# Packing the turned values of two head groups, one sum matmul, and a later setup in a fused attention and feed-forward kernel

## The chip, the cores and the metric

The kernel runs on one core of one Trainium2 chip. The metric is the device time of one execution in microseconds (us), less is better. The engines are TensorE (PE in the profile, with its weight loads as PEld), VectorE (DVE), ScalarE (ACT), GpSimd (POOL) and SyncE (SP), which issues all DMAs here.

## The reference

Sixteen batches of 256 tokens with 128 features go through one post-norm transformer layer. Everything is float32 at the interfaces.

```python
def _genetic_fitness(g):                       # per head, T x 8
    corr = g g^T / (|g_i| |g_j| + 1e-8)
    corr = (corr * m + 1) / 2                  # m: causal band of 128
    denom = mean_j(corr) + 0.5
    fit = 1 / (denom * sum_i(1 / denom))       # the sum runs over the 256 tokens
    return softmax(where(m, corr * fit, -1e10))
# attention
g, v = x @ Wg.T + bg, x @ Wv.T + bv            # 16 heads of 8
x = layernorm(x + (fitness(g) @ v) @ Wo.T + bo)
# feed-forward: inputs and weights quantised to FP4 in blocks of 16
gate, up = fp4(x) @ fp4(w_gate).T, fp4(x) @ fp4(w_up).T     # 352 wide
x = layernorm(x + fp4(silu(gate) * up) @ fp4(w_down).T)
```

## The kernel before

Each engine has its own instruction stream, written out by hand, and the streams meet in semaphores. All streams run the same loop of rounds, `t` from -3 to 20. Round `t` computes the scores and exponentials of batch `t`, and beside them the early steps of batches `t+1` to `t+3` and the late steps of batches `t-1` to `t-4`. So the order in each stream is fixed: an instruction that waits holds everything behind it on its engine.

For a batch the steps are these. TensorE makes genes and values in bank WA (L787, and the gene bias by L789); ScalarE squares and copies them (L603, L608); VectorE sums to squared lengths and seeds a reciprocal square root (`seed`), which GpSimd refines in twelve small steps (`newton`, L437 to L444). VectorE scales the genes (`gh`), GpSimd and VectorE split them into two 16-bit halves (A16: L495, L1159). TensorE takes window sums (L799), VectorE turns these into `rden`, the reciprocal of the denominator for 2 x 16 columns (two token tiles of 16 heads). TensorE sums `rden` over the tokens (L819, two matmuls that accumulate the two tiles), VectorE takes the reciprocal (`rtot`, L1095) and the fitness, which scales the genes again (Bf, L1109; B16: L488, L1125). A16 and B16 are turned on TensorE (L716) and copied to AT and BT by ScalarE (L570, L582).

The scores of two heads at a time go to bank S (L668 adds the mask, L672 the products), ScalarE takes exponentials to Pm (L531). `values(x, c)` multiplies the Pm of head group `c` (four heads) with gv (L689): each head has 9 columns that matter (8 values and a column of ones for the sum) in a slot of 32, and the result is turned, with heads along the partitions. Groups 0 and 1 lie beside each other in bank OT as two regions of 256 columns, so do 2 and 3, and ScalarE copies each pair to OTs (`values_out`, L544, 512 columns). `values_back` turns them back with the picking matrix `pick`, one matmul for each group and token tile, into bank WA (L703), where VectorE divides (L1146, L1152). Then come the projection (L828), the first norm, FP4 quantisation of x, gate and up (L709, L710), tanh, quantisation of h, its turn (L743), down (L761) and the second norm.

Setup before the first round: TensorE computes the bias rows and a combined output bias (L640 to L642) and VectorE copies them to `bias`; GpSimd splits this into three bf16 rows (L393 to L404) and builds masks and `pick`. The FP4 quantisation of the three weight matrices (`weights_to_scale` to `weights_scaled` on VectorE, over 1120 columns) and their turn on TensorE (`turn_weights`) stand in rounds -2 and -1.

## Time and profile before

| | us |
|---|---|
| median of 3 runs | 452.44 (451.97 to 454.86) |
| the profiled execution | 455.05 |
| span in its profile, first to last instruction | 453.3 |
| PE busy in the span | 363.7 (80%) |
| DVE busy | 273.4 (60%) |
| ACT busy | 229.6 (51%) |
| POOL busy | 179.1 (40%) |
| mean granted TensorE clock | 0.882 of full speed |

The span is what the profile shows; 1.75 us of the profiled execution lie outside it. The granted clock has two levels, 0.5 (1.2 GHz) and 1.0 (2.4 GHz). Times in rows are microseconds from the start of the span. A matmul in float32 is shown as two passes, each with its own weight load, so eight picking matmuls stand as x16.

### The profile page before, as it was taken

To read this page: it belongs to the slowest core of one execution; us is meant where nothing else is said; L and a number is where in the kernel's file an instruction comes from. 1 tells how busy PE (TensorE), PEld (TensorE's weight loads), DVE (VectorE), ACT (ScalarE), POOL (GpSimd) and SP (SyncE) were. 2 spreads that over 40 slices of the span, in tenths; PEclk is the share of its full clock that TensorE was granted. 3 is DMA by queue.
4 is the path that set the end of the run, shared out by engine and by line. 5 is a ranking of instruction groups with operands and counts; after the bars stand their busy time and mean duration, and the time that the engine had idled before them with its cause. 6 is when DMAs were issued, how large, how long until landed. Compare 5 with 4: busy or idle time off the path is not lost.

```text
span 453.3 us, 9200 instructions
## 1 busy us (share of the span) xinstructions
PE 363.7 (80%) x3121; PEld 226.8 (50%) x3121; DVE 273.4 (60%) x804; ACT 229.6 (51%) x498; POOL 179.1 (40%) x464
## 2 busy tenths in 40 slices
PE   1425887798898989898898989898999989966552
PEld 1214344454656565656465656555656564654242
DVE  0565123335547776768686768575656657888661
ACT  1101555627346657575757475657274647633121
POOL 4743230404224636353645354626152323325241
PEclk9999589959589999899999899989696969998555
DMA  3100000000000101010101010100000000000000
GB/s 88 35 1 23 2 13 0 25 1 23 1 21 5 37 1 37 1 36 4 35 1 36 3 35 1 37 1 25 0 25 2 25 0 25 2 12 13 12 2 25
DMA packets 12407, 7.66 MB, mean 17 GB/s; under 512 B 1027, under 2 KB 12357, under 8 KB 12357
## 3 DMA queue, kind: packets, MB, share of 16 engines
q1 hardware_dynamic: 12356, 7.03, 5.5%
q8 instruction: 26, 0.43, 0.4%
q14 instruction: 25, 0.20, 0.2%
HBM read 4.93 MB, written 2.10 MB: 16 GB/s over the span
## 4 chain that ended last, share of the span: by engine, by line
PE 71%; ACT 11%; issue 7%; DVE 6%; POOL 3%; DMA 0%; SPq 0%; ACTq 0%; POOLq 0%; DVEq 0%
PE OT L689 12%; PE S L668 9%; PE WA L703 8%; PE WD L761 7%; PE S L672 7%; PE WC L709 6%; PE WD L710 5%; PE WB L716 4%; PE WA L787 4%; ACT AT L570 3%; ACT Pm L531 3%; ACT xaT L596 2%; PE WB L828 2%; PE WA L819 2%; ACT y L537 1%
## 5 line engine op out<-in xcount | busy, mean ns | idle before, releaser
L531 ACT ACTIVATE Pm<-S 128x384 f32<-128x384 f32 x256 | 111.9, 492 | 107.9 <-PE S L672 107.2
L668 PE MATMUL S<-mask,ident 128*128 128x384 f16 x256 | 68.9, 354 | 10.0 <-ACT Pm L531 8.4
L461 POOL TENSOR_TENSOR hq<-hm,hs 128x352 f32<-128x352 f32 x32 | 25.2, 788 | 96.9 <-DVE hm L1036 96.8
L689 PE MATMUL OT<-Pm,gv 128*32 128x256 f32 (+1 forms) x1024 | 60.6, 359 | 0.0
L672 PE MATMUL S<-BT,AT 32*128 32x256 f16 (+1 forms) x512 | 45.7, 258 | 0.0
L1012 DVE SCALAR_TENSOR_TENSOR hh<-th,WC 128x352 f32<-128x352 f32 x32 | 16.7, 522 | 44.2 <-ACT th L549 44.2
L689 PEld LDWEIGHTS OT<-Pm,gv 128*32 128x32 f32 x1024 | 28.3, 115 | 22.5 <-issue 7.8
L709 PE MATMUL WC<-wguT,xaT 128*128 128x352 f32 x64 | 29.5, 544 | 11.7 <-ACT xaT L596 7.1
L672 PEld LDWEIGHTS S<-BT,AT 32*128 32x128 f16 x512 | 14.6, 94 | 45.8 <-issue 45.8
L703 PE MATMUL WA<-pick,OTs 128*128 128x36 f32 x256 | 36.7, 306 | 0.0
L668 PEld LDWEIGHTS S<-mask,ident 128*128 128x128 f16 x256 | 19.0, 100 | 34.2 <-issue 16.3
L703 PEld LDWEIGHTS WA<-pick,OTs 128*128 128x128 f32 x256 | 35.6, 222 | 0.2 <-issue 0.2
L437 POOL TENSOR_TENSOR nt<-seed 128x32 f32<-128x32 f32 x16 | 4.8, 303 | 77.4 <-DVE seed L982 77.4
L761 PE MATMUL WD<-wdT,hqT 128*128 128x128 f32 (+1 forms) x192 | 33.8, 341 | 1.8 <-ACT hqT L577 1.8
L544 ACT ACTIVATE OTs<-OT 128x512 f32<-128x512 f32 x32 | 19.2, 599 | 29.0 <-PE OT L689 29.0
L761 PEld LDWEIGHTS WD<-wdT,hqT 128*128 128x128 f32 (+1 forms) x192 | 30.3, 245 | 5.6 <-ACT hqT L577 2.8
L716 PE MATMUL WB<-ident,B 128*128 128x128 f16 x128 | 11.5, 241 | 24.0 <-ACT AT L570 17.2
L1125 DVE TENSOR_TENSOR B<-Bf,B 128x512 f16<-128x512 f32 x16 | 11.1, 692 | 27.0 <-POOL B L488 27.0
L787 PE MATMUL WA<-wgv,xT 128*128 128x256 f32 x64 | 22.2, 481 | 5.2 <-issue 4.2
L710 PE MATMUL WD<-wguT,xaT 128*128 128x352 f32 x64 | 26.0, 490 | 0.0
L1146 DVE RECIPROCAL orec<-WA 128x32 f32<-128x32 f32 x16 | 5.7, 358 | 33.6 <-PE WA L703 33.6
L455 POOL TENSOR_TENSOR hn<-h,hrn 128x352 f32<-128x352 f32 x32 | 25.1, 793 | 1.4
(142 smaller groups left out, 714.5 us busy)
## 6 DMA issues: line engine op xcount, KB each, us to landing
xT<-x_turned_dram SPq DMA_DIRECT2D x16, 128.0 KB, 2.3
x_res<-x_dram SPq DMA_DIRECT2D x16, 128.0 KB, 2.2
out_dram<-yo SPq DMA_DIRECT2D x16, 128.0 KB, 2.1
wf<-w_down_dram SPq DMA_DIRECT2D x1, 176.0 KB, 2.6
wgv<-wgv_dram SPq DMA_DIRECT2D x1, 128.0 KB, 2.0
wf<-w_gate_dram SPq DMA_DIRECT2D x1, 128.0 KB, 2.2
wf<-w_up_dram SPq DMA_DIRECT2D x1, 128.0 KB, 2.2
woT<-wo_dram SPq DMA_DIRECT2D x1, 64.0 KB
```

Of the source, the lines that this page charges most:

```text
L455: pool.tensor_tensor(b3(hn[:, k]), b3(h[:, k]), bc(hrn[:, k], QB), ALU.mult).then_inc(s_hn, 1)
L461: pool.tensor_tensor(b3(hq[:, k, 0:I]), b3(hm[:, k]), bc(hs[:, k], QB), ALU.mult).then_inc(s_hq, 1)
L531: act.activation(Pm[:, group % PR, hd % 4, :], S[:, (H * x + hd) % 3, 0:SCW], ACT.Exp, scale=1.0 / ZS).then_inc(s_exp, 1)
L668: pe.matmul(S[:, bank, 0:SCW], ident16[:, :], mask16[:, :], start=True, stop=False)
L672: i = pe.matmul(S[:, bank, q0:q1], AT[r:r + 32, x % 2, c, kt * P:(kt + 1) * P], BT[r:r + 32, x % 2, c, T - (q1 - q0):T], start=False, stop ...
L689: i = pe.matmul(OT[VP * g:VP * (g + 1), col + T - (q1 - q0):col + T], gv[:, x % GVR, kt, H + 4 * c + g, :], Pm[:, (GROUPS * x + c) % PR, g ...
L703: i = pe.matmul(WA[:, o:o + 4 * OW], OTs[:, c // 2, T * (c % 2) + n * P:T * (c % 2) + (n + 1) * P], pick[:, :, :].rearrange("p g e -> p (g ...
L709: pe.matmul(WC[:, 0:I], lhs, wguT[:, 0:I], start=True, stop=True)
L710: pe.matmul(WD[:, 0:I], lhs, wguT[:, I:2 * I], start=True, stop=True).then_inc(s_gu, 1)
L716: i = pe.transpose(WB16[:, c * T + n * P:c * T + (n + 1) * P], src[:, n * H + 4 * c:n * H + 4 * c + 4].rearrange("p h r d -> p (h r d)"), ...
L761: i = pe.matmul(WD[:, k * D:(k + 1) * D], hqT[0:kn, k, n * P:(n + 1) * P], wdT[0:kn, n, :], start=(n == 0), stop=(n == 2))
L787: pe.matmul(WA[:, k * 2 * D:(k + 1) * 2 * D], xT[:, (t + 3) % 2, k * P:(k + 1) * P], wgv[:, :], start=(k == 0), stop=False)
```

## The change

Three things are done. First, the two groups of a pair now share one region of 256 columns in OT. For an odd group the stationary operand is taken from `gv_flat` 9 columns earlier, so that its 9 columns land on rows 9 to 17 of each slot of 32, and all four accumulating steps of the pair form one sum; the zeros of gv are set one head further. `values_out` copies 256 columns, and `values_back` does one matmul with 72 columns for each pair and token tile: four for each batch in place of eight with 36.

Second, `rden` is summed over tokens with both tiles side by side in one matmul of 32 columns, and VectorE adds the two halves in an instruction of its own (`tot`) before the reciprocal. The aggregation of the first norm now stands ahead of the fitness.

Third, the setup is moved. The gene matmuls of batch 0 are TensorE's first work; for batches 0 and 1 the bias is added by a float32 matmul from `bgrow`. The bias rows are computed in round -3, and split by GpSimd in round -2 (`constants`) after its half of A16 of batch 0; the fill of gv stands in round -1. The weights are scaled at the end of round -1, quantised at the end of round 0, and turned in round 1, in two parts.

```diff
@@ setup, SyncE and GpSimd @@
+            sp.dma_start(xT[:, 0, :], x_turned[0]).then_inc(ld_x[0], 16)
             sp.dma_start(wgv[:, :], wgvT).then_inc(ld_w, 16)
-            sp.dma_start(xT[:, 0, :], x_turned[0]).then_inc(ld_x[0], 16)
-            sp.dma_start(bgrow[:, :], bg.rearrange("(a n) -> a n", a=1)).then_inc(ld_b, 16)
+            sp.dma_start(bgrow[:, :], bg.rearrange("(a n) -> a n", a=1)).then_inc(ld_w, 16)
...
-                pool.memset(gv[:, :, :, H:2 * H, OW:VP], 0.0).then_inc(c_pool, 1)
+                pool.memset(gv[:, :, :, H - 1:2 * H, OW:VP], 0.0).then_inc(c_pool, 1)
...
-                if t == -2:
-                    values_rest()
...
+                if t == -2:
+                    constants()
+                if t == -1:
+                    values_rest()
@@ ScalarE @@
-                act.activation(OTs[:, half, :], OT[:, :], ACT.Copy).then_inc(s_ot, 1)
+                act.activation(OTs[:, half, :], OT[:, 0:T], ACT.Copy).then_inc(s_ot, 1)
@@ TensorE, values and values_back @@
-                        i = pe.matmul(OT[VP * g:VP * (g + 1), col + T - (q1 - q0):col + T],
-                                      gv[:, x % GVR, kt, H + 4 * c + g, :], Pm[:, (GROUPS * x + c) % PR, g, q0:q1],
-                                      start=(kt == 0), stop=(kt == 1))
+                        at = VP * (2 * H * (NT * (x % GVR) + kt) + H + 4 * c + g) - OW * (c % 2)
+                        i = pe.matmul(OT[VP * g:VP * (g + 1), T - (q1 - q0):T], gv_flat[:, at:at + VP],
+                                      Pm[:, (GROUPS * x + c) % PR, g, q0:q1],
+                                      start=(kt == 0 and c % 2 == 0), stop=(kt == 1 and c % 2 == 1))
...
-                    for c in range(GROUPS):
-                        o = (n * H + 4 * c) * OW
-                        i = pe.matmul(WA[:, o:o + 4 * OW], OTs[:, c // 2, T * (c % 2) + n * P:T * (c % 2) + (n + 1) * P],
-                                      pick[:, :, :].rearrange("p g e -> p (g e)"), start=True, stop=True)
+                    for half in range(2):
+                        o = (n * H + 8 * half) * OW
+                        i = pe.matmul(WA[:, o:o + 8 * OW], OTs[:, half, n * P:(n + 1) * P],
+                                      pick[:, :, :, :].rearrange("p c g e -> p (c g e)"), start=True, stop=True)
@@ TensorE, rounds @@
+                if t == 1:
+                    turn_gate_up_weights()
...
+                    if t < -1:
+                        pe.matmul(genes, onesf[0:1, :], bgrow[:, :].rearrange("p (a d) -> p a d", a=1)
+                                  .to_broadcast([1, NT, D]), start=False, stop=True).then_inc(s_gv, 1)
...
-                    for k in range(NT):
-                        i = pe.matmul(WA[:, 0:H], onesf[:, :], rden[:, k * H:(k + 1) * H],
-                                      start=(k == 0), stop=(k == NT - 1))
-                    i.then_inc(s_sum, 1)
+                    pe.matmul(WA[:, 0:NT * H], onesf[:, :], rden[:, :], start=True, stop=True).then_inc(s_sum, 1)
@@ VectorE @@
-                    dve.reciprocal(rtot[:, :], WA[:, 0:H]).then_inc(s_fit, 1)
+                    dve.tensor_reduce(tot[:, :], WA[:, 0:NT * H].rearrange("p (n h) -> p h n", n=NT), AX.X, ALU.add)\
+                        .then_inc(s_fit, 1)
...
+                if t == -1:
+                    weights_to_scale()
+                if t == 0:
+                    weights_exponent()
+                    weights_round()
+                    weights_grid()
                     weights_scaled()
-                if t == -1:
-                    weights_turned()
+                if t == 1:
+                    down_weights()
```

TensorE at the start of the program. Before, the bias rows stand ahead of the genes of batch 0:

```order
L640 MATMUL WC<-bgrow,onesf 128x128 [waits c_dve,ld_b,c_pool]
L641 MATMUL WC<-woT,bvrep 128x128
L642 MATMUL WC<-borow,onesf 128x128
L787 MATMUL WA<-wgv,xT 128x256 [waits ld_x0,c_pool,ld_w]
L787 MATMUL WA<-wgv,xT 128x256
L789 MATMUL WA<-bias16,ones16 128x2x128
```

Now, the same place:

```order
L813 MATMUL WA<-wgv,xT 128x256 [waits ld_x0,ld_w,c_pool]
L813 MATMUL WA<-wgv,xT 128x256
L817 MATMUL WA<-bgrow,onesf 128x2x128
L654 MATMUL WC<-bgrow,onesf 128x128 [waits c_dve,ld_b]
L655 MATMUL WC<-woT,bvrep 128x128
L656 MATMUL WC<-borow,onesf 128x128
```

The genes went ahead of the bias rows, and their last matmul reads `bgrow` instead of the split bias.

VectorE at the turn from round 0 to round 1. `wq_u`, `wq_m` and `wf` belong to the weights, `seed` to batch 3, the rest to batch 2. Before:

```order
L982 TENSOR_SCALAR seed<-seed 128x32 [waits s_n2]
L1095 RECIPROCAL rtot<-WA 128x16 [waits s_sum]
L1100 TENSOR_TENSOR fit<-rden,rtot 128x32 [waits s_fit]
L1109 SCALAR_TENSOR_TENSOR Bf<-gh,fit 128x256 [waits s_Blo,s_fit]
L1125 TENSOR_TENSOR B16<-Bf,B16 128x64x8 [waits s_B,s_Bhi]
```

Now:

```order
L1016 TENSOR_SCALAR seed<-seed 128x32 [waits s_n2]
L976 TENSOR_SCALAR wq_u<-wf 128x1120 [waits c_dve]
L979 TENSOR_SCALAR wq_u<-wq_u 128x1120 [waits c_dve]
L983 TENSOR_TENSOR wq_m<-wf,wq_u 128x1120 [waits c_dve]
L987 TENSOR_TENSOR wq_m<-wq_m,wq_u 128x1120 [waits c_dve]
L991 TENSOR_TENSOR wf<-wq_m,wq_s 128x1120 [waits s_setup]
L1129 TENSOR_REDUCE tot<-WA 128x16 [waits s_sum]
L1135 RECIPROCAL rtot<-tot 128x16 [waits s_fit]
L1140 TENSOR_TENSOR fit<-rden,rtot 128x32 [waits s_fit]
L1147 SCALAR_TENSOR_TENSOR Bf<-gh,fit 128x256 [waits s_Blo,s_fit]
L995 COPY wguT<-WC 128x352 [waits c_pe]
```

Five instructions on the weights came between the seed of batch 3 and the fitness of batch 2.

TensorE in round 1, from its first pair of scores on. Before:

```order
L672 MATMUL S<-BT,AT 128x128 x2
L668 MATMUL S<-mask16,ident16 128x384 [waits s_exp]
L668 MATMUL S<-mask16,ident16 128x384
L672 MATMUL S<-BT,AT 128x256 x2
```

Now:

```order
L691 MATMUL S<-BT,AT 128x128 x2
L664 MATMUL WC<-identf,wf 128x128 [waits c_dve]
L664 MATMUL WC<-identf,wf 128x128
L664 MATMUL WC<-identf,wf 128x96
L664 MATMUL WD<-identf,wf 128x128 x2
L664 MATMUL WD<-identf,wf 128x96
L687 MATMUL S<-mask16,ident16 128x384 [waits s_exp]
```

The turn of the gate and up weights, which waits for the last of the five instructions above, came between two pairs of scores.

## Rows read from the trace of the kernel before

**Rows 1.** The chain that ended last: shares of the span by line.

```profile
by line: PE OT L689 12.4%; PE S L668 9.3%; PE WA L703 7.5%; issue 6.8%; PE WD L761 6.6%; PE S L672 6.6%; PE WC L709 6.3%; PE WD L710 4.6%; PE WB L716 4.5%; PE WA L787 3.9%; ACT AT L570 3.2%; ACT Pm L531 2.8%; ACT xaT L596 1.9%; PE WB L828 1
```

**Rows 2.** Waits of TensorE: us in total, times, longest.

```profile
PE WB L716 <- ACT AT L570: 17.2, 14, 1.3
PE WC L709 <- ACT xaT L596: 7.1, 14, 0.5
```

**Rows 3.** The chain in order of time: start, us, what.

```profile
160.60 1.03 ACT AT L570
...
162.30 1.76 PE WA L703 x16
...
165.55 1.53 PE WD L761 x12
...
181.84 1.03 ACT AT L570
...
314.00 1.03 ACT AT L570
...
316.04 3.37 PE WA L703 x16
...
339.95 1.03 ACT AT L570
```

**Rows 4.** Timeline of round 6: start, us, instruction [idle before, releaser].

```profile
170.43 0.60 ACT L544 ACTIVATE OTs<-OT 128x512 f32<-128x512 f32 x1 [1.79 <-PE OT L689]
...
171.57 0.86 PE L709 MATMUL WC<-wguT,xaT 128*128 128x352 f32 x2 [0.50 <-ACT xaT L596]
...
172.15 0.41 ACT L603 ACTIVATE gsq<-WA 128x256 f32<-128x256 f32 x1
...
173.55 0.62 PE L819 MATMUL WA<-rden,onesf 128*128 128x16 f32 x4
...
178.22 0.52 DVE L1012 SCALAR_TENSOR_TENSOR hh<-th,WC 128x352 f32<-128x352 f32 x1 [1.55 <-ACT th L549]
...
180.31 0.87 ACT L531 ACTIVATE Pm<-S 128x384 f32<-128x384 f32 x2 [0.57 <-PE S L672]
```

**Rows 5.** Stretches: length, busy PE, PEld, DVE, ACT, POOL, then granted clock.

```profile
90.00:100.00 10.00, 9.36 (x53) 6.26 (x53) 3.24 (x9) 2.76 (x6) 0.00 (x0) 0.50 0.01 2
...
366.40:373.20 6.80, 6.80 (x42) 4.25 (x43) 4.54 (x13) 1.79 (x3) 0.00 (x0) 0.50 0.00 0
```

**Rows 6.** Timeline of the opening.

```profile
11.48 2.05 PE L787 MATMUL WA<-wgv,xT 128*128 128x256 f32 x4 [4.25 <-issue]
...
16.18 0.25 POOL L444 TENSOR_TENSOR rn<-nt,seed 128x32 f32<-128x32 f32 x1
...
17.54 1.36 POOL L444 TENSOR_TENSOR rn<-nt,rn 128x32 f32<-128x32 f32 x1
...
21.32 3.21 POOL L423 MEMSET gv<- 128x3680 f32 x1
...
24.58 0.61 POOL L495 CAST A<-gh 128x512 f16<-128x512 f32 x1
...
35.77 0.61 POOL L488 CAST B<-Bf 128x512 f16<-128x512 f32 x1
...
44.60 0.50 PE L668 MATMUL S<-mask,ident 128*128 128x384 f16 x2 [1.42 <-DVE wdT L968]
```

**Rows 7.** DMA issues: engine, size, us from issue to landing.

```profile
wgv<-wgv_dram SPq DMA_DIRECT2D x1, 128.0 KB, 2.0
```

**Rows 8.** Timeline around the start of round 1.

```profile
62.90 0.18 DVE L982 TENSOR_SCALAR seed<-seed 128x32 int32<-128x32 int32 x1
...
65.42 0.50 PE L668 MATMUL S<-mask,ident 128*128 128x384 f16 x2 [0.64 <-ACT Pm L531]
```

**Rows 9.** DVE busy on the tile wq_u, then on wq_m, by stretch.

```profile
14.00:20.50 6.50, 1.49 (x2) 1.00 0.20 61
25.50:32.00 6.50, 3.90 (x3) 1.00 0.00 0
```

More of the change, by code:

```diff
@@ L94, in layer @@
         win16 = sb("win16", [P, SCW], F16)
-        pick = sb("pick", [P, 4, OW])
+        pick = sb("pick", [P, 2, 4, OW])
         mhalf = sb("mhalf", [P, 4])
@@ L139, in layer @@
         Pm = sb("Pm", [P, PR, 4, SCW])
-        OTs = sb("OTs", [P, 2, 2 * T])
+        OTs = sb("OTs", [P, 2, T])
         orec = sb("orec", [P, NT * H])
@@ L416, in _, with constants @@
                                        pattern=[[sign, P]], channel_multiplier=-sign).then_inc(c_pool, 1)
-            pool.tensor_copy(pick[:, :, :], identf[:, :].rearrange("p (g e) -> p g e", e=VP)[:, :, 0:OW])\
-                .then_inc(c_pool, 1)
+            band(win16, 0.0)
+            pool.wait_ge(c_pool, 6)
+            pool.tensor_copy(ident16[:, :], identf[:, :]).then_inc(c_pool, 1)
+            def constants():
+                pool.memset(ones16[:, :], 1.0).then_inc(c_pool, 1)
+                pool.memset(bias16[:, :], 0.0).then_inc(c_pool, 1)
+                pool.memset(mhalf[:, :], -0.5).then_inc(c_pool, 1)
+                pool.memset(mask16[:, :], 0.0).then_inc(c_pool, 1)
+                pool.wait_ge(c_pool, 14)
+                band(mask16, MASKED)
+                for k in range(2):
+                    pool.tensor_copy(pick[:, k], identf[:, :].rearrange("p (g e) -> p g e", e=VP)
+                                     [:, :, k * OW:(k + 1) * OW]).then_inc(c_pool, 1)
+                pool.wait_ge(c_dve, 2)
+                pool.tensor_copy(biasp[:, :], bias[:, :]).then_inc(c_pool, 1)
+                pool.wait_ge(c_pool, 20)
+                pool.tensor_copy(bias16[0:1, :], biasp[0:1, :]).then_inc(c_pool, 1)
+                pool.tensor_tensor(biasr[:, :], bias[:, :], biasp[:, :], ALU.subtract).then_inc(c_pool, 1)
+                pool.wait_ge(c_pool, 22)
+                pool.tensor_copy(biasp[:, :], biasr[:, :]).then_inc(c_pool, 1)
+                pool.wait_ge(c_pool, 23)
+                pool.tensor_copy(bias16[32:33, :], biasp[32:33, :]).then_inc(c_pool, 1)
+                pool.wait_ge(c_pool, 24)
+                pool.tensor_tensor(biasr[:, :], biasr[:, :], biasp[:, :], ALU.subtract).then_inc(c_pool, 1)
+                pool.wait_ge(c_pool, 25)
+                pool.tensor_copy(bias16[64:65, :], biasr[64:65, :]).then_inc(c_pool, 1)
+                pool.wait_ge(c_pool, 26)
             def values_rest():
                 pool.memset(gv[:, :, :, H:2 * H, HD:OW], 1.0).then_inc(c_pool, 1)
-                pool.memset(gv[:, :, :, H:2 * H, OW:VP], 0.0).then_inc(c_pool, 1)
+                pool.memset(gv[:, :, :, H - 1:2 * H, OW:VP], 0.0).then_inc(c_pool, 1)
                 pool.memset(hq[:, :, I:HP], 0.0).then_inc(c_pool, 1)
@@ L635, in _, with biases, turn_gate_up_weights @@
         def _(pe):
[L637 to L646 removed]
+            def biases():
+                pe.wait_ge(ld_b, 16 * 3)
+                pe.wait_ge(c_dve, 1)
+                pe.matmul(WC[:, 0:D], onesf[0:1, :], bgrow[:, :], start=True, stop=True)
+                pe.matmul(WC[:, D:2 * D], bvrep[:, :], woT[:, :], start=True, stop=False)
+                pe.matmul(WC[:, D:2 * D], onesf[0:1, :], borow[:, :], start=False, stop=True).then_inc(c_pe, 1)
+            def turn_gate_up_weights():
                 pe.wait_ge(c_dve, 11)
@@ L788, in _ @@
                                   start=(k == 0), stop=False)
-                    pe.matmul(WA[:, :].rearrange("p (n k) -> p n k", n=NT)[:, :, 0:D], ones16[:, :],
-                              bias16[:, 0:D].rearrange("p (a d) -> p a d", a=1).to_broadcast([P, NT, D]),
-                              start=False, stop=True).then_inc(s_gv, 1)
+                    genes = WA[:, :].rearrange("p (n k) -> p n k", n=NT)[:, :, 0:D]
+                    if t < -1:
+                        pe.matmul(genes, onesf[0:1, :], bgrow[:, :].rearrange("p (a d) -> p a d", a=1)
+                                  .to_broadcast([1, NT, D]), start=False, stop=True).then_inc(s_gv, 1)
+                    else:
+                        if t == -1:
+                            pe.wait_ge(c_pool, 26)
+                        pe.matmul(genes, ones16[:, :],
+                                  bias16[:, 0:D].rearrange("p (a d) -> p a d", a=1).to_broadcast([P, NT, D]),
+                                  start=False, stop=True).then_inc(s_gv, 1)
+                    if t == -3:
+                        biases()
                 if live(t + 2):
```

120 lines of the change are left out of this document (50 added, 70 removed).

## Prediction

> **What bounds the kernel now.** I read the chain that ended last first: its shares by line [rows 1]. The reader is to see that TensorE's lines (PE) fill most of it, and that the picking matmuls, which the change halves, are the third largest with 7.5% of 453.3, 34 us. Then the waits of TensorE [rows 2]: only two come back in nearly every batch, 14 times each. It waits for ScalarE's copy of AT, 1.3 us at most, and for the copy xaT, 0.5 us. Everything else of a batch is TensorE's own row of instructions. Then the chain in order of time [rows 3]: a batch lasts 181.84 - 160.60 = 21.24 us from one copy of AT to the next, and one batch 339.95 - 314.00 = 25.95. The picking took 1.76 us in the first and 3.37 in the second. The granted clock explains that [rows 5]: between 60 and 380 us there are eight stretches in which it is 0.5, the 1.2 GHz level (the rows show the first and the last of the eight), in sum 56 us. Each begins within 2 us of the place where TensorE waits for AT, turns B16 and picks. The batch of 25.95 us held one of 10 us, so a microsecond at the low level costs (25.95 - 21.24) / 10 = 0.47 us. Last the timeline of a round [rows 4] and of the opening [rows 6, 8]. The opening takes 44.6 us before the first scores, and nothing in it is long work: it is one chain through all engines.
>
> **Picking, 16 passes to 8.** One pass takes 1.76 / 16 = 110 ns with 36 columns [rows 3]. The down matmuls with 128 columns take 1.53 / 12 = 127 ns for a pass [rows 3]. So 72 columns cost 110 to 127 ns, and I take 117, nearer to 36 columns. For a batch at the high level that is 1.76 - 8 x 0.117 = 0.82 us less. Over the span half of the 34 us goes, 17, and about 1 comes back for the longer pass: **-16.0** (bounds -17.0 and -14.8). It lies on the path whole: before it TensorE has just waited for AT, behind it stand `values(t, 0)` and scores whose inputs were ready. VectorE's division waits for the picking and moves with it.
>
> **Values, same count.** The 16 passes of L689 stay, but for odd groups the weights start 9 columns off a slot. I take 0. No row has such an offset. A pass of L689 takes 12.4% of the span by 1024, 55 ns [rows 1]. A loss is bounded by the pace of a pass with a full weight load, 110 ns: 32 passes in the two odd groups of a batch add at most 1.8 us. A gain I exclude, since size and count are the same.
>
> **Sum of 1/denominator.** Four passes of 16 columns take 0.62 us [rows 4]; two passes of 32 columns remain. At the 110 ns pace that saves 0.22 us for a batch, more at the low level: **-3.8** for 16 (bounds -3.0 and -4.8). VectorE gets one small instruction more (I take 0.2 us; a seed step on as many columns takes 0.18 [rows 8]). It is free: VectorE idles 1.55 us ahead of its gate step in the same round [rows 4], and B16 is made by GpSimd only after its own work for the next batch.
>
> **values_out, 512 to 256 columns.** The copy takes 0.60 us, a ScalarE instruction on 256 columns from the same kind of bank 0.41 [rows 4]. The first of the two copies of a batch stands right ahead of xaT, for which TensorE waits 0.50 us, 14 times [rows 2, 4]: 0.2 x 14 = **-2.8** (bounds -1.5 and -3.1). The second is worth nothing: ScalarE idles 0.57 us behind it, until TensorE's scores come [rows 4], and so the wait for AT stays as it is.
>
> **The opening.** Gene matmuls start at 11.48 now, behind bias rows, their copy and GpSimd's split [rows 6]. They will need only x, wgv and `bgrow`, the first three of SyncE's loads; with 2.0 us for one of them [rows 7] and an issue of the third before 2 us I estimate a start at 3.9: -7.6. The float32 bias matmul costs two passes of 256 columns, +0.7 against the bf16 one. GpSimd's refinement ran beside VectorE's weight work, where one step took 1.36 us in place of 0.25 [rows 6]; without it I take -2.0 (bounds -1.1 and -3.0). The fill of gv, 3.21 us ahead of A16 [rows 6], goes behind it: -3.4 with its neighbours. So A16 of batch 0 starts at 24.6 - 12.3 = 12.3 us. Then GpSimd does the constants ahead of refining batch 1: the split, for which TensorE now waits 4.25 us [rows 6], and masks and pick, which I put at 1.6. They end at 12.3 + 0.6 + 5.9 = 18.8. The refinement is twelve steps, and four take 17.54 - 16.18 = 1.36 us [rows 6], so 4.1 in all and B16 of batch 0 at about 23 in place of 35.77 [rows 6]: -12.7. The wait for turned weights ahead of the first scores, 1.42 us [rows 6], goes, and two passes of the sum, 0.3: first scores at 30.2, **-14.4**.
>
> Part of this is handed back. (a) Scaling the weights at the end of round -1, which I put at 3.8 us of VectorE (two instructions of the 1.3 us kind [rows 9] and three short ones), puts B16 of batch 1 about 0.5 us behind its use: +0.5. (b) At the end of round 0 VectorE does five weight instructions, 1.49 + 3.90 = 5.4 us [rows 9], behind the seed of batch 3 (before: 62.90 + 0.18 = 63.08 [rows 8]). They end at 63.1 + 5.45 = 68.5 on the old time scale. TensorE comes to the turn of the gate and up weights at 65.42 - 0.64 = 64.8 [rows 8] and has to wait 3.7 us; behind it everything of round 1 is queued. With 1.1 us for the six transposes (0.8 by the 127 ns pass, twice that at the low level) it takes up the next scores at 69.6 in place of 65.42: +4.2. (c) The turn of the down weights stands on TensorE's full path: +0.4. (d) After that wait I expect a stretch at 1.2 GHz which that place has not now. With 0.47 us for each of some 6 us (the eight run from 3 to 13): +3.0 (bounds 0 and +6). Together the opening gives -14.4 + 0.5 + 4.2 + 0.4 + 3.0 = **-6.3**, bounds -10 and 0.
>
> In (b) GpSimd refines batch 3 at the same time, and its steps will be drawn out as the 1.36 us step was. That is hidden: its B16 of batch 2 is used some 10 us later. In rows, VectorE has not paid for the meeting. The Trainium skill (SBUF — State Buffer, SBUF: two separate sides) says that VectorE with two SBUF inputs and GpSimd exclude each other for a whole instruction, and whichever starts first holds the ports, so VectorE could be the one blocked. By that rule up to twelve steps of 0.25 us would lengthen the train, and the sum would be 3 us less of a gain; the trace bears out the blocking, but only on GpSimd's side.
>
> **Clock in the steady rounds.** The place where all eight slow stretches begin gets denser: the picking takes half as long with twice the columns in a pass. I expect fewer stretches: with six instead of eight some 14 us less at the low level, 6.6 us, of which the picking's own term holds a part: **-4** (bounds -12 and +6).
>
> **The sum.** -16.0 - 3.8 - 2.8 - 6.3 - 4.0 = -32.9. The profiled execution took 455.05 us, 453.3 of it the span; it lies 2.6 above the median of 452.44. I carry the difference over to the median: 452.4 - 32.9 = 419.5, so **420 us**, 7% less. A change of 1% either way is about what a measurement of this kernel can tell from none. A batch at the high level should take 21.24 - 0.82 - 0.22 - 0.2 = 20.0 us.
>
> **Rivals.** (1) *The opening gives nothing*: the weight train, drawn out by GpSimd, and longer stretches at 1.2 GHz in rounds 0 to 3 eat what the early start won. For it speaks that TensorE gets a wait of 3.7 us where it was dense; against it the sizes above. Opening 0 and no change of clock behind it: 452.4 - 22.6 = 430, or up to 436 with +6. Chance 0.17. (2) *The slow stretches nearly vanish* after round 3: 56 us at 0.47 are 26, of which the picking's term holds 3: up to 12 more than my -4 is plausible, 408. Chance 0.17. The Trainium skill (TensorE: Matmul & The Clock Gate, What's actually happening) has the clock as a gate that activity opens; the row of stretches agrees, and by it both this rival and (1) are open, since the change makes one place denser and puts one wait in. (3) *Shifted weights load slowly*: 1.8 us for each of 16 batches, +29, which cancels the gain: 449. Nothing in the profile speaks for it; chance 0.03. (4) *Slower*: the clock falls in every batch at the wait for AT, since the batch has less TensorE work around waits that stay. If each of 16 batches had a stretch of 12 us, 192 us in place of 56, that is 136 x 0.47 = +64 against -29 for the rest: 487. It decides from 29 / 0.47 = 62 us more at the low level. Against it stands that the waits get shorter. Chance 0.03. That the change does not do what it says would show as 256 picking passes or first scores after 40 us; the instruction order excludes it.
>
> **How the numbers follow.** My forecast, 412 to 428, has 0.60, (1) 0.17, (2) 0.17, (3) and (4) 0.03 each. The predicted time is that of the first. The range runs from 407, which takes in most of (2), to 434, which takes in most of (1); outside are (3), (4) and the ends. Faster by over 1% (below 447.9): the first three cases and little of (3), 0.94, and 0.01 of (3). Within 1%: the rest of (3), 0.02. Slower: (4), 0.03.
>
> **What would show it.** In the profile after: picking x128 with 0.9 to 1.0 us for x8 at the high level; the sum as x32; OTs copies of about 0.4 us and the wait for xaT at 0.3; the wait for AT unchanged at 1.3 us; first scores at 29 to 32 us; a wait of 3 to 5 us of TensorE at the turn of the gate and up weights; five to seven slow stretches between there and the end of the steady rounds. Wrong it would be if the values passes got longer than 55 ns each, if VectorE's train made TensorE wait elsewhere too, or if the count of slow stretches changed by more than three.

## The result and the profile after

The changed kernel takes 415.09 us in the median (412.52 to 417.64, 4 runs) against 452.21 (449.47 to 454.86, 4 runs) before. The ratio is 0.916, with a 95% interval from 0.911 to 0.921: 8.4% less. The prediction was 420 us, range 407 to 434. The profiled execution took 414.54 us, 412.8 of it the span, at a mean granted clock of 0.889 (0.882 before). One execution of a kernel can come out 1.5 to 3% longer than its shortest one; the ratios below leave such executions out, and for two variants (picking with 36 columns, copy of 512 elements), where two of the four are of that kind, no ratio is given and the two shorter ones are compared.

The chain that ended last in the changed kernel, its shares by line (the view of [rows 1]):

```profile
by line: PE OT L708 12.7%; PE S L687 8.8%; PE WC L728 6.9%; PE S L691 6.4%; PE WD L787 6.1%; issue 5.8%; PE WD L729 5.0%; PE WB L735 4.5%; PE WA L813 3.9%; PE WA L722 3.7%; ACT AT L583 3.5%; ACT Pm L544 2.8%; PE WB L862 2.0%; ACT xaT L609 1
```

The picking (now L722) fell from 7.5% to 3.7%, from 34.0 to 15.3 us. The values matmuls (L708, before L689) went from 56 to 52 us.

TensorE's waits: us in total, times, longest.

```profile
PE WB L735 <- ACT AT L583: 17.2, 14, 1.3
PE WC L728 <- ACT xaT L609: 4.2, 14, 0.4
PE WC L664 <- DVE wf L991: 4.1, 1, 4.1
```

Against [rows 2] the wait for AT is unchanged to the tenth, the one for xaT is 0.2 us shorter each time, and behind the first scores there is one large new wait of 4.1 us, for the weights.

The chain in order of time, around two steady rounds and a slow place (start, us, what):

```profile
142.07 1.03 ACT AT L583
143.76 0.90 PE WA L722 x8
146.15 1.53 PE WD L787 x12
162.03 1.02 ACT AT L583
...
183.65 0.90 PE WA L722 x8
187.02 2.07 PE WD L787 x12
```

A batch lasts 162.03 - 142.07 = 19.96 us (19.93 for most) in place of 21.23 [rows 3], and eight picking passes take 0.90 us, 112 ns each.

The timeline of that round:

```profile
150.14 0.86 PE L708 MATMUL OT<-Pm,gv 128*32 128x256 f32 x16
151.07 0.39 ACT L557 ACTIVATE OTs<-OT 128x256 f32<-128x256 f32 x1 [1.82 <-PE OT L708]
151.99 0.86 PE L728 MATMUL WC<-wguT,xaT 128*128 128x352 f32 x2 [0.29 <-ACT xaT L609]
153.97 0.41 PE L855 MATMUL WA<-rden,onesf 128*128 128x32 f32 x2
155.83 0.18 DVE L1129 TENSOR_REDUCE tot<-WA 128x16 f32<-128x32 f32 x1
```

Against [rows 4] the copy takes 0.39 us instead of 0.60, the wait behind it 0.29 instead of 0.50, the sum 0.41 instead of 0.62, and VectorE has its new instruction of 0.18 us. The 16 values passes for odd and even groups alike take 0.86 us.

The opening and the turn to round 1:

```profile
3.57 2.05 PE L813 MATMUL WA<-wgv,xT 128*128 128x256 f32 x4 [3.57 <-DMA bgrow<-bg_dram]
5.55 1.22 PE L817 MATMUL WA<-bgrow,onesf 1*128 1x256 f32 x2
12.77 0.61 POOL L504 CAST A<-gh 128x512 f16<-128x512 f32 x1 [0.52 <-DVE gh L1170]
23.27 0.61 POOL L497 CAST B<-Bf 128x512 f16<-128x512 f32 x1
30.08 0.49 PE L687 MATMUL S<-mask,ident 128*128 128x384 f16 x2
32.82 1.33 DVE L972 TENSOR_TENSOR wf<-wf,wq_r 128x1120 f32<-128x1120 f32 x1
32.90 1.36 POOL L455 TENSOR_TENSOR rn<-nt,rn 128x32 f32<-128x32 f32 x1
37.11 1.01 PE L735 MATMUL WB<-ident,B 128*128 128x128 f16 x8 [0.57 <-DVE B L1162]
53.03 1.32 DVE L991 TENSOR_TENSOR wf<-wq_m,wq_s 128x1120 f32<-128x1120 f32 x1
54.41 0.85 PE L664 MATMUL WC<-identf,wf 128*128 128x128 f32 x3 [4.07 <-DVE wf L991]
```

The first scores start at 30.08 us, 14.5 earlier than in [rows 6]. The wait at L664 is the price of quantising the weights late. The row of 1.36 us on GpSimd beside VectorE's 1.33 is the meeting of [rows 6], at its new place.

The clock is 0.5, the 1.2 GHz level, in six stretches between 61 and 330 us, in sum some 22 us when whole slices of 0.4 us are counted (five of about 3, one of 6.4; 24 us with their edges), and in one of 6.8 us ahead of them, right behind the new wait. It is also low from 31 to 45 us, and from 366 us to the end, where the batches run out. Two of the stretches, and a long stretch between others (length, then busy PE, PEld, DVE, ACT, POOL, then granted clock, as in [rows 5]):

```profile
51.60:58.40 6.80, 3.99 (x30) 2.21 (x31) 5.46 (x11) 0.87 (x2) 4.98 (x11) 0.50 0.01 2
...
184.80:188.20 3.40, 3.40 (x28) 1.88 (x21) 3.30 (x10) 1.09 (x3) 1.06 (x2) 0.51 0.02 5
120.00:180.00 60.00, 55.28 (x555) 33.68 (x554) 48.53 (x151) 41.14 (x93) 31.78 (x83) 1.00 0.08 21
```

Where the 40.5 us between the two spans went: the second AT copy on the chain (60.51 after, 69.09 before) is 8.6 us earlier. From it to the copy 13 batches on (327.62 after, 363.31 before) there are 27.1 us less, and 13 x (21.23 - 19.93) = 16.9 of these are the pace of a batch. The other 10.2 go with the clock: between the same two copies 49 us at the low level before, 22 after, so 0.38 us for each. The end gives 4.8. These are two single executions, and the low level differs between executions of one kernel: the mean granted clock of the four runs of the changed kernel goes from 0.879 to 0.896.

### The profile page after: what moved, and what is told of

Its sections match the earlier page's. It is cut to its first block, busy times and chain, and to the rows that moved or that the text cites. A ratio compares the mean times of both kernels' runs of the same rounds, so it can differ in the third digit from the quotient of the medians.

```text
span 412.8 us, 8902 instructions
## 1 busy us (share of the span) xinstructions
PE 337.1 (82%) x2963; PEld 201.6 (49%) x2963; DVE 279.6 (68%) x820; ACT 222.7 (54%) x498; POOL 182.0 (44%) x465
## 4 chain that ended last, share of the span: by engine, by line
PE 67%; ACT 11%; DVE 9%; issue 6%; POOL 5%; DMA 0%; ACTq 0%; SPq 0%; POOLq 0%; DVEq 0%
PE OT L708 13%; PE S L687 9%; PE WC L728 7%; PE S L691 6%; PE WD L787 6%; PE WD L729 5%; PE WB L735 5%; PE WA L813 4%; PE WA L722 4%; ACT AT L583 3%; ACT Pm L544 3%; PE WB L862 2%; ACT xaT L609 2%; ACT y L550 2%; PE WC L799 1%
## 5 line engine op out<-in xcount | busy, mean ns | idle before, releaser
L687 PE MATMUL S<-mask,ident 128*128 128x384 f16 x256 | 67.2, 346 | 7.9 <-ACT Pm L544 7.8
L708 PE MATMUL OT<-Pm,gv 128*32 128x256 f32 (+1 forms) x1024 | 59.6, 354 | 0.0
L708 PEld LDWEIGHTS OT<-Pm,gv 128*32 128x32 f32 x1024 | 28.0, 114 | 22.6 <-issue 9.6
L691 PEld LDWEIGHTS S<-BT,AT 32*128 32x128 f16 x512 | 14.5, 93 | 44.2 <-issue 44.2
L787 PE MATMUL WD<-wdT,hqT 128*128 128x128 f32 (+1 forms) x192 | 32.1, 329 | 1.7 <-ACT hqT L590 1.7
L787 PEld LDWEIGHTS WD<-wdT,hqT 128*128 128x128 f32 (+1 forms) x192 | 28.7, 234 | 5.3 <-ACT hqT L590 2.9
L466 POOL TENSOR_TENSOR hn<-h,hrn 128x352 f32<-128x352 f32 x32 | 27.3, 859 | 1.3
L562 ACT ACTIVATE th<-WC 128x352 f32<-128x352 f32 x32 | 14.9, 464 | 21.7 <-PE WD L729 21.6
L557 ACT ACTIVATE OTs<-OT 128x256 f32<-128x256 f32 x32 | 12.3, 386 | 25.6 <-PE OT L708 25.6
L813 PE MATMUL WA<-wgv,xT 128*128 128x256 f32 x64 | 20.6, 453 | 3.6 <-DMA bgrow<-bg_dram 3.6
L481 POOL TENSOR_TENSOR rstd<-ve,mhalf 128x2 f32<-128x2 f32 x32 | 23.0, 719 | 0.0
L735 PEld LDWEIGHTS WB<-ident,B 128*128 128x128 f16 x128 | 7.9, 103 | 27.4 <-ACT AT L583 21.3
```

The costliest lines, as they stand in the source:

```text
L466: pool.tensor_tensor(b3(hn[:, k]), b3(h[:, k]), bc(hrn[:, k], QB), ALU.mult).then_inc(s_hn, 1)
L481: pool.tensor_tensor(r[:, :], ve[:, :], mhalf[:, 0:NT], ALU.pow).then_inc(s_out, 1)
L687: pe.matmul(S[:, bank, 0:SCW], ident16[:, :], mask16[:, :], start=True, stop=False)
L691: i = pe.matmul(S[:, bank, q0:q1], AT[r:r + 32, x % 2, c, kt * P:(kt + 1) * P], BT[r:r + 32, x % 2, c, T - (q1 - q0):T], start=False, stop ...
L708: i = pe.matmul(OT[VP * g:VP * (g + 1), T - (q1 - q0):T], gv_flat[:, at:at + VP], Pm[:, (GROUPS * x + c) % PR, g, q0:q1], start=(kt == 0 a ...
L735: i = pe.transpose(WB16[:, c * T + n * P:c * T + (n + 1) * P], src[:, n * H + 4 * c:n * H + 4 * c + 4].rearrange("p h r d -> p (h r d)"), ...
```

## Experiments

**The three parts alone.** Each was put into the kernel before by itself.

```diff
@@ pack only @@
-                        i = pe.matmul(OT[VP * g:VP * (g + 1), col + T - (q1 - q0):col + T],
+                        i = pe.matmul(OT[VP * g:VP * (g + 1), T - (q1 - q0):T], gv_flat[:, at:at + VP],
...
-                    for c in range(GROUPS):
+                    for half in range(2):
@@ sum only @@
-                    for k in range(NT):
-                        i = pe.matmul(WA[:, 0:H], onesf[:, :], rden[:, k * H:(k + 1) * H],
-                                      start=(k == 0), stop=(k == NT - 1))
+                    pe.matmul(WA[:, 0:NT * H], onesf[:, :], rden[:, :], start=True, stop=True).then_inc(s_sum, 1)
@@ setup only @@
+                if t == -2:
+                    constants()
...
+                if t == 0:
+                    weights_exponent()
```

> The kernel before with the packing alone: shared OT region, copies of 256 columns, four picking matmuls of 72 columns per batch. Theory (three separate terms): picking passes 16 to 8 and the shorter copies take about 19 + 3 us off TensorE's path, and a few us come from fewer 1.2 GHz stretches: 425 to 431 us, x128 picking passes at about 112 ns. Rival (the clock is the main gain): the number of slow stretches falls from eight to four or fewer with packing alone, and the time to 415 to 422 us. Rival (shifted weights are slow): L689 passes above 60 ns and 440 us or more.

Measured: 423.41 us (420.89 to 430.35), ratio 0.934, 95% interval 0.930 to 0.937. A batch at the high level lasts 20.46 us, 0.77 less than 21.23. The time lies between the ranges of the theory and of the rival with the clock: 16 x 0.77 = 12.3 us of the 29 are pace, so more than half of what packing alone gained goes with the clock. The mean granted clock of its four shorter runs is 0.914 to 0.922, against 0.875 to 0.889 in the kernel before; the profile is that of the longest, 430.35 us, and only the pace is read from it.

> The kernel before with the sum of 1/denominator alone in one matmul of 32 columns and the extra VectorE instruction. Theory: -3 to -4 us, 448 to 450, with the copies of AT and the waits of TensorE unchanged. Rival (the added VectorE instruction and the later aggregation are seen by GpSimd): no change or up to 3 us slower, with a new wait of TensorE at the turn of B16 for VectorE.

Measured: 440.54 us (437.94 to 443.82), ratio 0.972 [0.965, 0.979]. A batch lasts 21.00, 0.23 less. That is 16 x 0.23 = 3.7 us, the 3 to 4 that were expected; the rest of the 12 goes with the clock, since between 60 and 380 us its profile has 37.6 us at the low level in place of 56. Nobody expected that part.

> The kernel before with the setup moved alone (genes of batch 0 first, constants in round -2, weights at the ends of rounds -1 and 0, turned in round 1). Theory: first scores at 30 us in place of 44.6, 4 us of waiting at the turn of the gate and up weights, 6 to 10 us less in all: 442 to 447. Rival (handed back later through slow stretches in rounds 1 to 4): under 4 us less, above 448.

Measured: 445.81 us (443.36 to 447.51), ratio 0.987 [0.984, 0.990]. A batch lasts 21.23 as before, AT of batch 2 is copied at 60.48, 8.6 us earlier than before, and the wait for the turned weights is 3.9 us.

The three savings sum to 29 + 12 + 7 = 48 us, and together they gave 37. The opening adds up, and so does the pace, but for 0.31 us a batch that packing alone loses (below); the parts that are clock do not.

**Weights ahead of the window products.** The changed kernel, with the five weight instructions of round 0 earlier in VectorE's row:

```diff
+                if t == 0:
+                    weights_exponent()
+                    weights_round()
+                    weights_grid()
+                    weights_scaled()
                 if live(t - 2):
                     quant_x(t - 2, 6)
...
-                if t == 0:
-                    weights_exponent()
...
```

> The changed kernel with VectorE's five weight instructions of round 0 put ahead of the window products of batch 2, into the idle time in the middle of the round, in place of the round's end. Theory (the wait of 4.1 us for the turned weights is on the path and causes the slow stretch behind it): the wait goes, the stretch at 1.2 GHz from 51.6 to 58.4 shortens or goes, 4 to 8 us less than 415: 407 to 411. Rival (the time is lost to something later in round 1 anyway, the copy of AT or B16 of batch 2): under 2 us less.

Measured: 406.78 us (402.91 to 409.34), ratio 0.896 [0.891, 0.902], 8.3 us less than the changed kernel. TensorE turns the weights without a wait, and the stretch of 6.8 us at 1.2 GHz behind it is gone:

```profile
50.88 0.52 PE L664 MATMUL WC<-identf,wf 128*128 128x128 f32 x3
```

The same row took 0.85 us in the changed kernel, behind 4.07 of idle time. AT of batch 2 comes 5.3 us earlier, and that is what the wait and its stretch cost here; the prediction had 4.2 + 3.0. The other 3 of the 8.3 us come later and are not shown to be due to the wait: the clock differs there too.

**Picking with 36 columns again.** The changed kernel, same packed data, 16 passes:

```diff
-                        i = pe.matmul(WA[:, o:o + 8 * OW], OTs[:, half, n * P:(n + 1) * P],
-                                      pick[:, :, :, :].rearrange("p c g e -> p (c g e)"), start=True, stop=True)
+                        for c in range(2):
+                            i = pe.matmul(WA[:, o + 4 * c * OW:o + 4 * (c + 1) * OW], OTs[:, half, n * P:(n + 1) * P],
+                                          pick[:, c].rearrange("p g e -> p (g e)"), start=True, stop=True)
```

> The changed kernel with the picking done as 16 passes of 36 columns for a batch, as before the change, on the same packed data. Everything else as changed. The prediction's step: a pass costs about 110 ns whatever it holds, so eight passes more cost 0.82 to 0.86 us at the high level: fast batch 20.8 in place of 19.95, picking x16 at 1.76, 415.1 + 13.5 = 429 with the clock unchanged. On the clock: theory A, that fewer passes at this place are what removed slow stretches, expects some 25 us more at the low level and 440; rival B, that any change of pace shifts them by chance, expects 420 to 440 with no link to the place. If the packing's whole gain came from the shorter copies and not from the picking, it would be 417.

Measured: 433.59 us (428.69 to 436.64). The chain, in order of time:

```profile
151.86 1.76 PE WA L723 x16
```

A batch lasts 20.79, 0.86 more than 19.93: the eight passes at 107 ns. Over 16 batches that is 13.8 us. The two shorter runs, 428.69 and 430.83, lie 13.6 and 15.7 us above 415.09, so pace accounts for nearly all of it. From 61 to 350 us the profile (of 430.83) shows about 34 us at the low level, between the 22 of the changed kernel and the 47 that theory A wanted, but the mean granted clock of these two runs, 0.911 and 0.895, is no lower than the changed kernel's 0.879 to 0.896. The passes taken out at this place bring pace; that they bring clock as well is not shown. A pass of 72 columns costs what one of 36 does, 112 against 110 ns. The Trainium skill (TensorE: Matmul & The Clock Gate, LDWEIGHTS) has the time of a weight load go by its columns, P / 1.2 ns, which makes an estimate of 107 ns for the 128 columns loaded here. The two rows agree, at 110 and 112 ns.

**The copy at 512 elements again.** The changed kernel:

```diff
-                act.activation(OTs[:, half, :], OT[:, 0:T], ACT.Copy).then_inc(s_ot, 1)
+                act.activation(OTs[:, half, :].rearrange("p (r t) -> p r t", r=2),
+                               OT[:, 0:T].rearrange("p (r t) -> p r t", r=1).to_broadcast([P, 2, T]), ACT.Copy).then_inc(s_ot, 1)
```

> The changed kernel with each copy of OT to OTs at 512 elements again (the 256 columns written twice). The prediction's step: 0.2 us for a batch through the wait for xaT, 14 times, so fast batch 20.15 and 415.1 + 2.8 = 418 with the clock unchanged. Theory A for the clock (it is the wait for AT that counts, and that stays at 1.28) expects 415 to 421. If the wait for xaT counts too, which goes from 0.3 back to 0.5 us, slow stretches come back, 425 or more. If the copy was never on the path: 415.

Measured: 418.14 us (411.64 to 425.02). The total doesn't show the cost of the copy: the two shorter runs, 411.64 and 413.32, are no longer than the changed kernel. They have the clock higher, at 0.923 and 0.907. The pace does show it: a batch lasts 20.14 us, 0.21 more, and the wait for xaT is back:

```profile
PE WC L729 <- ACT xaT L610: 7.1, 14, 0.6
```

**VectorE's xn ahead of the division.** Pack only gave 0.77 us for a batch, but the picking (0.86) and the copy (0.21) should give 1.07. In the timeline of pack only TensorE begins the turn of xm 0.55 us behind that of attn, where the changed kernel needs 0.28 (148.21 and 148.49 in its rows): 0.27 us are lost there (start, us, instruction):

```profile
163.16 0.78 POOL L458 TENSOR_TENSOR hn<-h,hrn 128x352 f32<-128x352 f32 x1
163.30 0.93 DVE L1069 SCALAR_TENSOR_TENSOR xn<-y,xr 128x256 f32<-128x256 f32 x1
...
164.48 0.28 DVE L1072 TENSOR_SCALAR xu<-xn 128x256 int32<-128x256 int32 x1
...
166.52 0.42 DVE L1082 TENSOR_TENSOR xm<-xn,xs 128x256 f32<-128x256 f32 x1
166.54 0.44 PE L776 MATMUL WC<-identf,attn 128*128 128x128 f32 x2
...
167.09 0.41 PE L784 MATMUL WC<-identf,xm 128*128 128x128 f32 x2
```

GpSimd's hn starts first, and VectorE's xn takes 0.93 us, to 0.28 us behind the end of hn. In the changed kernel the same two start together, xn takes its 0.36, and it is hn that is drawn out. VectorE doesn't go free there either: its next instruction, xu, falls into the rest of hn and takes 0.55 us in place of 0.28:

```profile
144.97 0.36 DVE L1100 SCALAR_TENSOR_TENSOR xn<-y,xr 128x256 f32<-128x256 f32 x1
144.97 1.00 POOL L466 TENSOR_TENSOR hn<-h,hrn 128x352 f32<-128x352 f32 x1
...
145.58 0.55 DVE L1103 TENSOR_SCALAR xu<-xn 128x256 int32<-128x256 int32 x1
...
148.21 0.44 PE L799 MATMUL WC<-identf,attn 128*128 128x128 f32 x2
...
148.49 0.38 PE L807 MATMUL WC<-identf,xm 128*128 128x128 f32 x2
```

So the meeting costs VectorE 0.93 - 0.36 = 0.57 us in pack only and 0.55 - 0.28 = 0.27 in the changed kernel, 0.30 less.

So in pack only I moved xn ahead of the reciprocal that waits for the picking:

```diff
+                if live(t - 2):
+                    quant_x(t - 2, 3)
                 if live(t - 1):
                     dve.wait_ge(s_ob, t)
                     dve.reciprocal(orec[:, :], o[:, :, HD]).then_inc(s_on, 1)
-                if live(t - 2):
-                    quant_x(t - 2, 3)
```

> The kernel before with the packing alone (423.4), and in VectorE's order the scaling of x (xn) ahead of the reciprocal that waits for the picking, not behind it. Packing alone gave 0.77 us for a batch where 1.0 was expected; there xn took 0.93 us instead of 0.36 beside GpSimd's hn, and TensorE waited 0.27 us for xm. Theory A: that meeting of VectorE and GpSimd cost the missing 0.25 us; with xn out of the way it comes back: xn at 0.36 to 0.45, no wait ahead of the turn of xm, fast batch 20.2, about 4 us less, 419. Rival B: the missing 0.25 us are the longer pass or the shorter copies' fault, fast batch stays 20.46 and the time 423. Reordering could also push the division later by up to 0.4 us, which has 1 us of room before the turn of attn.

Measured: 421.21 us (417.72 to 428.20), ratio 0.928 [0.920, 0.936], which overlaps that of pack only. The batch decides: 20.15 us, 0.31 less than 20.46, and the turn of xm again comes 0.28 us behind that of attn. xn still meets hn and ends 0.28 us behind it, but early, where there is room:

```profile
156.41 0.79 POOL L458 TENSOR_TENSOR hn<-h,hrn 128x352 f32<-128x352 f32 x1
156.82 0.66 DVE L1069 SCALAR_TENSOR_TENSOR xn<-y,xr 128x256 f32<-128x256 f32 x1
...
161.07 0.44 PE L776 MATMUL WC<-identf,attn 128*128 128x128 f32 x2
...
161.35 0.38 PE L784 MATMUL WC<-identf,xm 128*128 128x128 f32 x2
```

**The copy of AT first.** The changed kernel, on ScalarE:

```diff
                 exps(t, 2)
+                if live(t + 1):
...
+                    act.activation(AT[:, (t + 1) % 2].rearrange("p c t -> p (c t)"), WB16, ACT.Copy).then_inc(s_AT, 1)
                 if live(t - 2):
...
                     ln_apply(y, rstd1, nb1, y1[:, (t - 2) % YR], s_y1)
-                if live(t + 1):
...
-                    act.activation(AT[:, (t + 1) % 2].rearrange("p c t -> p (c t)"), WB16, ACT.Copy).then_inc(s_AT, 1)
```

> The changed kernel with one swap on ScalarE: the copy of AT for the next batch stands ahead of the two instructions that apply the first norm (0.87 us), not behind them. TensorE waits 1.28 us for that copy in 14 batches. Theory A: the wait is on the path with 0.64 us of it to be had (the copy would end at 142.44 in place of 143.09, and VectorE's half of B16 ends at 142.50): 14 x 0.64 = 9 us less, 406. Rival B: the norm comes 1.0 us later to VectorE, whose quantisation of x then ends behind TensorE's use of it (now xm ends within 0.2 us of its turn): a wait of about 0.6 us at the turn of xm takes the place of the one removed, and the time is 413 to 417. What the profile shows: wait for AT 0.6 in both, wait for xm 0.1 by A and 0.5 to 0.7 by B.

Measured: 402.23 us (400.91 to 403.77), ratio 0.888 [0.883, 0.893]. Both theories missed. The wait fell to 0.79 us, now for VectorE's half of B16, and TensorE begins the turn of xm 0.52 us behind that of attn in place of 0.28, a loss of 0.24 us, under half of what rival B wanted:

```profile
141.93 0.61 PE L735 MATMUL WB<-ident,B 128*128 128x128 f16 x8 [0.79 <-DVE B L1162]
...
146.99 0.44 PE L799 MATMUL WC<-identf,attn 128*128 128x128 f32 x2
...
147.51 0.41 PE L807 MATMUL WC<-identf,xm 128*128 128x128 f32 x2
```

A batch lasts 19.71, only 0.22 less, 3 us in all. But the time fell by 12.9, and the rest goes with the clock: after 80.8 us there is no stretch at 1.2 GHz until 357, and the mean granted clock is 0.931 in all four runs, against 0.879 to 0.896.

```profile
80.80:200.00 119.20, 108.85 (x1084) 64.13 (x1084) 91.65 (x278) 80.05 (x181) 56.85 (x149) 1.00 0.07 19
200.00:340.00 140.00, 131.38 (x1311) 79.14 (x1310) 117.09 (x351) 97.46 (x221) 68.91 (x167) 1.00 0.06 18
```

**The wait filled with matmuls for nothing.** To part the clock from the pace, the changed kernel gets more work in its wait, and nothing is made shorter:

```diff
+                if live(t - 1) and live(t + 1):
+                    pe.wait_ge(s_ot, 2 * (t - 1) + 2)
+                    for _ in range(6):
+                        pe.matmul(OT[:, T:2 * T], ident16[:, :], mask16[:, 0:T], start=True, stop=True)
                 if live(t + 1):
                     pe.wait_ge(s_AT, t + 2)
```

> The changed kernel with six matmuls more for a batch (128x256 in 16 bit, into the half of OT that is no longer used, read by nobody), right ahead of TensorE's wait for AT. That wait is 1.28 us in 14 batches and the six should take 0.7 to 1.0, so they fill it and the fast batch stays at 19.94. Theory A, that the slow stretches start at that wait because TensorE stands still there: they nearly vanish in the steady rounds (22 us at the low level now, then under 8), 415.1 - 7 = 408. Rival B, that what moved the stretches in the other runs was the length of a batch and not the wait: the stretches stay at 15 to 30 us and the time at 412 to 418.

Measured: 405.48 us (403.36 to 407.87), ratio 0.894 [0.887, 0.901], 9.6 us less than the changed kernel, with 84 matmuls more. A batch lasts 19.93 as in the changed kernel.

```profile
142.06 0.83 PE L773 MATMUL OT<-mask,ident 128*128 128x256 f16 x6
143.41 0.62 PE L735 MATMUL WB<-ident,B 128*128 128x128 f16 x8 [0.53 <-ACT AT L583]
```

Between 61 and 330 us one stretch of 6.4 us at the low level is left in place of six, and the mean granted clock of the four runs is 0.919 to 0.939, against 0.879 to 0.896. From the copy of AT for batch 2 to the last one the profiles have 260.5 us in place of 267.2, which is the whole difference of their spans (406.0 and 412.8). So theory A holds for this kernel as far as filling the wait goes, and B falls, since the batch has the same length. That the place matters, and not the added work by itself, is not shown: no run put the six matmuls elsewhere.

**The wait made longer.** The changed kernel, with a second copy ahead of that of AT:

```diff
+                    act.activation(dump[:, :], WB16[:, 0:512], ACT.Copy).then_inc(s_dump, 1)
                     act.activation(AT[:, (t + 1) % 2].rearrange("p c t -> p (c t)"), WB16, ACT.Copy).then_inc(s_AT, 1)
```

> The changed kernel with one copy more on ScalarE, 512 columns to a scratch tile, right ahead of the copy of AT: the wait of TensorE for AT goes from 1.28 to about 1.9 us in 14 batches. At the high level that costs 14 x 0.6 = 8.4 us, 423.5. Theory A, that this wait starts the slow stretches: more of them than the 22 us of steady rounds now, 50 us or more, so 436 or more. Rival B, that the wait isn't what starts them: 418 to 428.

Measured: 426.56 us (423.64 to 431.05), ratio 0.941 [0.930, 0.953].

```profile
257.90 0.62 PE L739 MATMUL WB<-ident,B 128*128 128x128 f16 x8 [1.78 <-ACT AT L587]
```

The wait is 1.78 us and a batch 20.41, 0.48 more, so 6.2 us in 13 batches. The time lies in the range of rival B, and the mean granted clock, 0.881 to 0.889, is about that of the changed kernel. The low level takes 32 us between 62 and 339, more than 22 but not 50, and all of it before 158. Here are the granted clocks in 40 equal slices of the span, of the changed kernel, with the wait filled, and with the wait longer, in this order:

```profile
PEclk9995869889899999998999999999799999975555
```

```profile
PEclk9999969699999999999999999999999999989555
```

```profile
PEclk9995865989596989999999999999999999987555
```

With the longest wait of the three the clock holds from 158 to 376 us. So theory A, put as "a longer wait, more stretches", does not hold for this run: filling the wait removed most of them, while lengthening it brought some more in the first batches and none later. In that run each begins within 1 us of the end of the wait, but which batches have one isn't told by the length of the wait alone.

**Together.** The early weights and the early AT copy in one kernel; and that with four matmuls for nothing ahead of the wait, since 0.8 us of it are left.

> The swap of the AT copy and the five weight instructions moved ahead of the window products of round 0, both on the changed kernel. The second alone gave 406.8. By theory A of the AT copy 398 (406.8 less 9), by its rival 405 to 408. If the stretches at 1.2 GHz answer to either, up to 8 us to each side.

Measured: 399.01 us (393.59 to 399.91), ratio 0.877 [0.870, 0.885].

> The weight train early, the copy of AT first and four matmuls for nothing ahead of the wait for AT, in one kernel. Without the four it gave 399.0, with three slow stretches after round 1 and a wait of 0.8 us for B16. If filling a wait keeps the clock high: 394 to 397; if its slow stretches come from elsewhere (the wait of 5.9 us in the opening, the end): 399. If the four matmuls outlast the wait: 401.

Measured: 395.40 us (393.47 to 395.85), ratio 0.872 [0.865, 0.879], the lowest median of all kernels here, 4.7% below the changed one. A batch lasts 19.69. After 46 us the first slice at the low level comes at 346, in the end of the kernel:

```profile
60.00:200.00 140.00, 130.62 (x1309) 77.16 (x1309) 106.12 (x323) 93.19 (x211) 65.24 (x171) 1.00 0.07 19
200.00:345.00 145.00, 137.67 (x1351) 82.44 (x1350) 120.75 (x363) 98.55 (x226) 71.29 (x174) 1.00 0.06 18
```

The intervals of the last two overlap, so that the four matmuls help here too is likely and not shown.

## Why the prediction was right

It was right in its sum because four of five terms held to 0.7 us, and short by 4.5 us (415.1 is 37.4 below the 452.4 that the prediction started from; 32.9 were forecast), most of it because of the fifth, the clock.

- **Picking.** 117 ns were taken for a pass of 72 columns, and it takes 112. Without the new form (16 passes of 36) a batch is 0.86 us longer, where 0.82 was forecast: 13.8 us at the high level, against 13.1. The shares of the chain fell by 18.7 us where the prediction said 16.0; the difference is passes that used to run at the low level.
- **Values.** Nothing, as taken: 0.86 us for x16 in odd and even groups. Rival (3) is excluded.
- **Sum.** 0.23 us for a batch alone, 0.22 forecast: -3.7 and -3.8. VectorE's new instruction takes 0.18, 0.2 forecast, and nobody waits for it.
- **Copy.** 0.21 us for a batch, 14 times: -2.9 against -2.8. The second copy and the wait for AT did not move, as said.
- **Pace.** 0.86 + 0.23 + 0.21 = 1.30 us, which is 21.23 - 19.93; forecast 20.0. The step on VectorE and GpSimd ("VectorE has not paid for the meeting") was right for the rows before and wrong as a rule: in pack only VectorE pays 0.57 us for a batch, and putting xn first gave 0.31 back. The changed kernel pays less, 0.27, in the instruction behind, since its xn comes to start no later than hn. Why hn starts 0.14 us ahead of xn in one and together with it in the other was not traced further. The Trainium skill (SBUF — State Buffer, SBUF: two separate sides) lets whichever starts first hold the shared ports until its instruction ends, where the VectorE instruction has two SBUF inputs. Both directions stand in the rows above, 0.93 for 0.36 and 1.00 for 0.79, and that xn ends 0.28 us behind hn whether it started 0.14 or 0.41 us after it agrees with the whole instruction.
- **Opening.** Setup only gained 7.0 us against the kernel before in the same series (452.8 to 445.8), -6.3 forecast. Step by step: genes at 3.57 (3.9), A16 at 12.77 (12.3), B16 at 23.27 (about 23), first scores at 30.08 (30.2), wait for batch 1's B16 0.57 (0.5), wait for the weights 4.1 (3.7). The stretch behind that wait was expected with some 6 us and has 6.8. What this wait and stretch hand back was taken too high, 7.2 against the 5.3 that the early weights got back, and the second AT copy on the chain accordingly comes 8.6 us earlier; the medians don't tell that from 7.0.
- **Clock.** This is the mis-sized term. With the picking at its high pace, pace and opening explain 13.8 + 3.7 + 2.9 + 7.0 = 27.4 of 37.4 us, and 10.0 are left for the clock, by the rows 10.2 between the two copies of AT. The prediction had 4, and 2.9 of slow picking in the term before it, 6.9 together. It took six stretches for eight, which is the number that came, and that is luck in part: they are shorter, 22 us in place of 42, and the reason given for them is not borne out by its own test. The reason was that the place where they begin gets denser by the faster picking; with the picking at 16 passes again the two shorter runs are longer by 13.6 and 15.7 us, of which 13.8 are pace, and hardly any clock comes back. The filled wait bears out that this place matters, but the wait made longer had no stretch from 158 to 376 us, and the sum alone, which does not touch the place, took 18 us of them away. So which batches fall to the low level depends on more than the length of this wait, and the cause of the 10 us stays open.

Of the rivals, (1) is refuted by setup only. (2) came halfway: what it would have been is the kernel with the wait filled, 405.5 us, 2.5 below its 408. (4) is refuted by the run that came nearest to it, a wait of 1.78 us in every batch without a slow stretch from 158 to 376 us.

The Trainium skill (TensorE: Matmul & The Clock Gate, What's actually happening) says that activity releases the throttle. That 84 matmuls for nothing save 9.6 us agrees; the run with the longer wait shows that the rule alone does not give the time. The prediction had the rows of the stretches agree already, but they can't tell: in the one at 90 us TensorE was busy for 9.36 of 10 us, at the low level.

## What to carry to other kernels

Where TensorE pauses at one place of every round, try to order its supplier earlier, or fill the wait with harmless matmuls: here either alone (12.9 and 9.6 us) was worth more than all the work that the change took off the path for the sum and the copy. That filling what is left after reordering helps again is likely and not shown. Merge small float32 matmuls that each load 128 columns of weights, since up to 72 columns their width was free here. When a setup step is moved behind the first batch, look for the one place where TensorE catches up with it, and put the step ahead of whatever work has room; and don't add up the measured gains of single parts where the clock is in them.

## What the runs showed of the hardware

- Work for nothing can shorten a kernel: six matmuls of 0.83 us in a pause of 1.28, in 14 batches, made 415.1 us into 405.5.
- The cost of the low level was 0.38 us for each us between the two copies of AT, less than the 0.47 of the batch that the prediction read. Perhaps TensorE waits in part of these stretches anyway; no run tested it.
- A two-input VectorE instruction of 0.36 us took 0.93 when a GpSimd instruction on SBUF had started 0.14 us earlier; it ended 0.28 us behind it, and did so too when it started 0.41 us after it. Started together with it, it took 0.36, GpSimd's 0.79 became 1.00, and VectorE's next instruction took 0.55 in place of 0.28.
- A float32 picking pass took 110 ns with 36 columns and 112 with 72.
